# An interaction-network kernel with a tower: loads of the first chunk in order of use, dummy passes on TensorE, and the tower's first layer started inside the last tiles

## What is computed

```python
def cin(x0, filters):                      # x0: (512, 32 fields, 32 d)
    prev, outs = x0, []
    for W in filters:                      # (1, 32*32, 128), then (1, 32*128, 128)
        z = einsum('bhd,bmd->bhmd', x0, prev).reshape(b, h*m, d)
        prev = relu(einsum('bpd,pn->bnd', z, W[0]))
        outs.append(prev)
    return sum(concatenate(outs, axis=1), axis=-1)          # (512, 256)
e = stack([tbl_f[ids[:, f]] for f in range(32)], axis=1)
h = concatenate([cin(e, (filter_0, filter_1)), dense_ctx], axis=1)   # (512, 272)
h = maximum(h @ W_top1 + b_top1, 0)        # 512 wide
h = maximum(h @ W_top2 + b_top2, 0)        # 256 wide
y = h @ W_top3                             # (512, 1)
```

## Time and profile before

| | |
|---|---|
| median of 3 runs | 954.28 us (953.75 to 955.1) |
| the profiled execution, own time | 953.77 us |
| its span in the trace | 951.8 us |
| PE, DVE, ACT, POOL busy | 91%, 80%, 80%, 71% of the span |

### The profile page before, as it was taken

The page is one execution under the profiler, slowest core; times in us unless marked ns, Lnnn a source line. Parts: engine busy times, 40 slices in busy tenths (PEclk is TensorE's granted clock), DMA queues, the critical chain, the costliest instruction groups (busy, mean ns, idle before and its releaser), DMA issues.

```text
span 951.8 us, 14370 instructions
## 1 busy us (share of the span) xinstructions
PE 867.6 (91%) x3572; PEld 660.0 (69%) x3572; DVE 760.1 (80%) x2380; ACT 763.3 (80%) x2559; POOL 680.0 (71%) x650
## 2 busy tenths in 40 slices
PE   0326999999999999999999999989999999999997
PEld 0114777777777777767777777767777777777763
DVE  0123798896889999887888999978898899998882
ACT  1316998987888989888888898888888889989852
POOL 6772888786878888885788788865666666676560
PEclk9999999999999999999999999999999999999999
DMA  9045666666666666666666666666566666665430
GB/s 263 12 125 154 153 149 152 144 151 162 149 156 158 149 144 140 155 143 149 158 147 162 160 147 148 140 153 143 145 158 152 147 159 149 140 143 109 84 73 0
DMA packets 57718, 133.84 MB, mean 141 GB/s; under 512 B 8785, under 2 KB 22321, under 8 KB 57538
## 3 DMA queue, kind: packets, MB, share of 16 engines
q0 software_dynamic: 22528, 69.22, 38.8%
q1 hardware_dynamic: 32178, 59.94, 19.6%
q10 hardware_dynamic: 2928, 3.76, 1.3%
HBM read 62.64 MB, written 5.24 MB: 71 GB/s over the span
## 4 chain that ended last, share of the span: by engine, by line
PE 82%; issue 9%; POOL 3%; ACT 2%; DVE 2%; another core or an unknown queue 1%; DMA 1%; POOLq 0%; DVEq 0%; ACTq 0%
PE ya L651 15%; PE ya L652 13%; PE ya L653 13%; PE yd L651 10%; PE yd L652 10%; PE yd L653 10%; PE acc L652 3%; PE acc L651 3%; PE acc L653 3%; ACT scaled L439 1%; POOL quarter L305 1%; PE acc L674 1%; PE ya L750 1%; DVE acc L568 1%
## 5 line engine op out<-in xcount | busy, mean ns | idle before, releaser
L439 ACT ACTIVATE scaled<-ya,emb 128x128 f32<-128x128 f32 x2304 | 645.9, 386 | 91.8 <-PE ya L653 84.1
L568 DVE SCALAR_TENSOR_TENSOR acc<-yd,emb,acc 128x128 f32<-128x128 f32 x1408 | 394.7, 343 | 51.6 <-PE yd L653 51.4
L651 PE MATMUL ya<-w_hi,prev_hi 128*128 128x512 f32 x576 | 243.2, 422 | 11.0 <-DVE prev_lo L534 5.4
L305 POOL TENSOR_TENSOR quarter<-scaled 128x512 f32<-128x512 f32 x128 | 197.9, 1546 | 71.0 <-DMA scaled<-scaled 51.4
L652 PE MATMUL ya<-w_lo,prev_hi 128*128 128x512 f32 x576 | 227.4, 395 | 0.0
L653 PE MATMUL ya<-w_hi,prev_lo 128*128 128x512 f32 x576 | 226.8, 394 | 0.0
L298 POOL DMA_DIRECT2D scaled<-scaled x128 | 117.6, 919 | 119.3 <-ACT scaled L439 112.6
L651 PE MATMUL yd<-w_hi,prev_hi 128*128 128x512 f32 x448 | 176.7, 394 | 1.8 <-DVE pooled_b L587 1.5
L652 PE MATMUL yd<-w_lo,prev_hi 128*128 128x512 f32 x448 | 175.7, 392 | 0.0
L653 PE MATMUL yd<-w_hi,prev_lo 128*128 128x512 f32 x448 | 175.7, 392 | 0.0
L651 PEld LDWEIGHTS ya<-w_hi,prev_hi 128*128 128x128 f32 x576 | 108.6, 189 | 83.0 <-ACT scaled L439 37.8
(11 more groups left out here) (68 smaller groups left out, 719.9 us busy)
## 6 DMA issues: line engine op xcount, KB each, us to landing
scaled<-scaled POOLq DMA_DIRECT2D x128, 512.0 KB, 8.1
xb<-xt_scratch SPq DMA_DIRECT2D x64, 512.0 KB
x<-xt_scratch SPq DMA_DIRECT2D x64, 192.0 KB
xm<-xt_scratch SPq DMA_DIRECT2D x32, 256.0 KB
emb<-in_tbl,idx POOLq DMA_INDIRECT x128, 4.0
scaled<-in_L_rec_filter SPq DMA_DIRECT2D x8, 256.0 KB
xt_scratch<-xt_stage SPq DMA_DIRECT2D x7, 256.0 KB
xt_scratch<-xt_stage SPq DMA_DIRECT2D x9, 128.0 KB
```

Of the source, the lines that this page charges most:

```text
L305: pool.tensor_tensor(four, piece[:, 0:C], piece[:, C:2 * C], ALU.add).then_inc(quartered, 1)
L439: op = act.activation(scaled[:, tile % PR, C * j + N * i:C * j + N * (i + 1)], ya[:, n % RA, N * i:N * (i + 1)], ACT.Copy, scale=scale_of( ...
L568: dve.scalar_tensor_tensor(after, y_part, scale_of(tile, HB * j + i), before, ALU.mult, ALU.add).then_inc(chained, 1)
L651: pe.matmul(dst, v_hi, m_hi, start=start, stop=False)
```

## The change

Five edits:

1. SP's loads for chunk 0 are issued as `xm`, `xb` first half, `xb` second half, then `x16`. Chunk 1 and the later ones keep their order.
2. DVE and ACT do the four steps k of chunk 0 first and the small product after them; before, it stood between the first product and the first split.
3. PE issues 20 dummy passes of 512 columns (`WARM`) on weights that are already there, between the turning of the first batch and layer 0 of chunk 0. PE's waits for the later weights' low parts and for the context's share come ahead of them.
4. The tower's first layer is taken apart. The `pooled0` part goes into the extra round of the loop: two of its four products behind the last `yd` bank of tile 125, the other two behind the third of four `yd` banks of tile 126. Behind those come three of the four turns of `pooled1_b` and the `pooled1` products of 384 of the 512 columns. After the last tile only one turn, an ACT copy of 128 columns and four products of 128 columns are left.
5. The PSUM banks change: `tower_ps` is `ya` 0, `ya` 1, `xm_ps` and `prod`, and the second layer goes to `yd`.

```diff
@@ @block.sync
-            load_l0(0)
+            load_xm(0)
+            load_xb(0, 0)
+            load_xb(0, 1)
+            load_x16(0)
@@ @block.vector
-            product(0, 0)
+            for k in range(KT):
+                product(0, k)
+                split_low(0, k)
             first_small()
-            for k in range(KT):
-                split_low(0, k)
-                if k + 1 < KT:
-                    product(0, k + 1)
@@ @block.scalar
-            split_high(0, 0)
+            for k in range(KT):
+                split_high(0, k)
             small_high(0)
-            for k in range(1, KT):
-                split_high(0, k)
@@ @block.tensor, ahead of layer 0 of chunk 0
-            pe.wait_ge(w_lo_ready, 2)
+            pe.wait_ge(w_lo_ready, 4)
+            pe.wait_ge(ctx_share_ready, H1 // P)
+            for _ in range(WARM):
+                pe.matmul(yd[:, 0, :], w1_hi[:, 0, :], w1_hi[:, 0:HB, :], start=True, stop=True)
@@ @block.tensor, new functions
+            def tower_pooled0(q):
+                pe.matmul(tower_ps[q], wt1_sb[:, 0, P * q:P * (q + 1)], pooled0[:], start=True, stop=False)
+
+            def tower_pooled1(tiles, part_no):
+                pe.wait_ge(summed1, DC * CPB * tiles.stop)
+                for t in range(tiles.start, tiles.stop):
+                    turn = pe.transpose(acc0[:, P * t:P * (t + 1)], pooled1_b[:, t, :], identity[:])
+                turn.then_inc(pooled1_turned, 1)
+                pe.wait_ge(pooled1_ready, part_no)
+                for q in range(H1 // P):
+                    mm = pe.matmul(tower_ps[q][:, P * tiles.start:P * tiles.stop], wt1_sb[:, 1, P * q:P * (q + 1)],
+                                   pooled1[:, tiles, :], start=False, stop=part_no == 2)
+                    if part_no == 2:
+                        mm.then_inc(tower_mm, 1)
@@ @block.tensor, in the loop, behind bank_d(tile, j)
+                            if c == CHUNKS and q < 2 and j == 2:
+                                if q == 0:
+                                    pe.wait_ge(a_used, a_number(CHUNKS - 1, DC - 1, AQ[DC - 1] - 1) + 1)
+                                    pe.wait_ge(folded0, 2 * BT)
+                                    pe.wait_ge(summed0, CHUNKS)
+                                tower_pooled0(2 * q)
+                                tower_pooled0(2 * q + 1)
+                                if q == 1:
+                                    tower_pooled1(slice(0, BT - 1), 1)
@@ @block.tensor, after the loop
-            pe.wait_ge(summed1, TILES)
-            for t in range(BT):
-                turn = pe.transpose(acc0[:, P * t:P * (t + 1)], pooled1_b[:, t, :], identity[:])
-            turn.then_inc(pooled1_turned, 1)
-            pe.wait_ge(folded0, 2 * BT)
-            for q in range(H1 // P):
-                pe.matmul(tower_ps[q], wt1_sb[:, 0, P * q:P * (q + 1)], pooled0[:], start=True, stop=False)
-            pe.wait_ge(pooled1_ready, 1)
-            for q in range(H1 // P):
-                pe.matmul(tower_ps[q], wt1_sb[:, 1, P * q:P * (q + 1)], pooled1[:],
-                          start=False, stop=True).then_inc(tower_mm, 1)
+            tower_pooled1(slice(BT - 1, BT), 2)
```

More of the change, by code:

```diff
@@ L43, in cin_tower @@
     PR = 4
+    WARM = 20
     EARLY = 3 * F // 4
@@ L115, in cin_tower @@
         bt2_sb = sb("bt2_sb", [P, H2 // P])
-        tower_ps = [yd[:, 0, :], yd[:, 1, :], yd[:, 2, :], prod[:]]
+        tower_ps = [ya[:, 0, :], ya[:, 1, :], xm_ps[:], prod[:]]
         h1 = scaled[:, 0, 0:4 * C].rearrange("p (q c) -> p q c", q=4)
@@ L486, in _ @@
                                 split_high(c + 2, 0)
-            act.wait_ge(pooled1_turned, 1)
-            act.activation(pooled1[:], acc0[:].rearrange("p (t b) -> p t b", t=BT), ACT.Copy).then_inc(pooled1_ready, 1)
+            for k, tiles in enumerate((slice(0, BT - 1), slice(BT - 1, BT))):
+                act.wait_ge(pooled1_turned, k + 1)
+                act.activation(pooled1[:, tiles, :], acc0[:].rearrange("p (t b) -> p t b", t=BT)[:, tiles, :],
+                               ACT.Copy).then_inc(pooled1_ready, 1)
             for q in range(H1 // P):
@@ L494, in _ @@
             for q in range(H2 // P):
-                act.activation(h2[:, q, :], ya[:, q, :], ACT.Relu,
+                act.activation(h2[:, q, :], yd[:, q, :], ACT.Relu,
                                bias=bt2_sb[:, q:q + 1]).then_inc(tower_relu, 1)
@@ L702, in _ @@
             layer0_rest(0)
-            pe.wait_ge(w_lo_ready, 4)
-            pe.wait_ge(ctx_share_ready, H1 // P)
+            def tower_pooled0(q):
[11 more added lines that the diff above has]
+                        mm.then_inc(tower_mm, 1)
             for c in range(CHUNKS + 1):
@@ L749, in _ @@
                 for q in range(H2 // P):
-                    mm = pe.matmul(ya[:, q, :], wt2_sb[:, t, P * q:P * (q + 1)], h1[:, t, :],
+                    mm = pe.matmul(yd[:, q, :], wt2_sb[:, t, P * q:P * (q + 1)], h1[:, t, :],
                                    start=t == 0, stop=t == H1 // P - 1)
```

## The result

The changed kernel took 965.47 us (960.73 to 966.39, 5 runs) against 954.28 before: ratio 1.0107, 95% interval 1.0081 to 1.0134. It is slower by 1.1%, where 947.8 was forecast. The same kernel, unedited, was measured again in two later sessions, on two different chips (the chip of the first result is not on record), and took **950.15 and 949.20 us**, with ratios of 0.9969 and 0.9966 to the kernel before beside it. Both are results; most of this document is about what lies between them.

The account below looks back on a forecast made before the run. Passes on TensorE (busy 91%) set the even stretch's pace, so only start and end could move: 953.77 - 5.0 (start) - 1.5 (end) = 947.3, as median 947.8 us. The range was 944.6 to 951.4.

Parts of the forecast that it names:

- What is late next: Start, behind layer 0 of chunk 0: `x16(1)` limits ACT's first scaling, which comes at 77.3, 5.7 us earlier than 83.01.
- If the 3.8 us stay: Start: the unexplained wait before `prev_hi` remains, and ACT's first scaling could start at 76.7, `x16(1)` aside.
- if they go: Start: the unexplained 3.8 us before `prev_hi` vanish, and ACT's first scaling could start at 72.9, `x16(1)` aside.
- The clock: Start, on PE: a lower clock level loses 0.7 us (0 to 1.5); the 20 dummies cost nothing and gain nothing.
- the sum of the start: Start up to the first scaling: 5.7 us earlier less 0.7 for the clock, a gain of 5.0 us.
- Steps of chunk 0: Start: four products 2.1 us apart, loads in time, layer 0's last pass at 68.7 instead of 75.00, 6.3 us earlier.
- `x16(1)` as the limit: Start of chunk 1: the load is issued at 67.3, POOL's small product starts at 75.3 and sets the first scaling.
- First scaling: Start, on ACT: the first scaling comes at 77.3 instead of 83.01.
- The end: Last tiles and tower: DVE held up 4.1 us, second layer 2.2 us earlier, gain 1.5 us (0.1 to 2.6).
- one such stretch: End, second layer: one low-clock stretch from 934.8 loses 0.3 us of the 2.2 gained, a second another 1.7.
- Of the rivals, the second: Start and end: the 3.8 us go, `x16(1)` is quick, PE keeps the upper clock; 944.2 at the least, chance 0.12.
- Rival 5: End: inserted products meet PE's lower clock, DVE held up 13 us instead of 4.1, result 956.7; chance 0.04.

Follow-up runs that it names:

- e1: The changed kernel with no dummy passes (WARM = 0) instead of 20; 951.41 us, ratio 0.9958 to the kernel before.
- e14: The kernel before, unedited, measured again in the fourth session; 954.15 us, ratio 1.0010.
- e2: The kernel before with only the 20 dummy passes added, PE's two waits moved ahead of them; 959.46 us, ratio 1.0042.
- e15: The changed kernel without its dummy passes, measured again in the fourth session; 950.54 us, ratio 0.9973.
- e18: The kernel before with only the 20 dummy passes and the two moved waits, measured again in the fifth session; 950.92 us, ratio 0.9992.
- e13: The changed kernel, unedited, measured again in the fourth session; 950.15 us, ratio 0.9969.
- e7: The changed kernel with its 20 dummies, POOL's 22 early gathers of the second batch moved from the start to among the tiles; 967.0 us, ratio 1.0126.
- e8: The changed kernel without dummies, POOL's 22 early gathers of the second batch moved from the start to among the tiles; 965.65 us, ratio 1.0123.
- e6: The changed kernel with 5 dummy passes of 512 columns instead of 20; 957.57 us, ratio 1.0019.
- e12: The changed kernel with its 20 dummy passes moved earlier, to about 34 us, ahead of the first batch's turns; 951.05 us, ratio 0.9969.
- e17: The changed kernel, unedited, measured a third time, in the fifth session; 949.2 us, ratio 0.9966.
- e9: The changed kernel without dummies and without the context's part of the tower (24 PE instructions less); 949.8 us, ratio 0.9963.
- e16: The changed kernel with its 20 dummies at 34 us, ahead of the turns, measured again in the fourth session; 950.41 us, ratio 0.9968.
- e3: The kernel before with only edits 4 and 5 (the tower taken apart, its banks); 953.53 us, ratio 0.9975.
- e5: The changed kernel with its 20 dummy passes cut from 512 to 128 columns; 965.99 us, ratio 1.0120.

## Why the prediction was wrong

**The steps that failed** are three, and they lean on the same unread wait. The first is in "What is late next": from the last pass to `prev_hi` the chain showed 3.8 us "for which I see no cause", and the sum carried them along as a constant or dropped them ("If the 3.8 us stay", "if they go"). A third case was missing: that they grow. They were a late increment of PE, and in the session of the result the changed kernel met it at PE's first step, with 16.2 us. The second is in "The clock": the dummies "cost nothing, and cover is the 8.7 us in which PE has nothing to do". The cover was there (PE is idle from 55.57 to 60.72), but in sessions of that kind the dummies cost 14 us (after against e1), and five of them or 20 short ones also cost something, so what they cost was not PE's time. The third is the sum of the start, which takes 77.3 from the measured 83.01. In 83.01 itself some 2.6 us of the 3.8 were on the path, so that half of the 5.0 us counted as the change's gain was not its own; this shows in the sessions without late increments, below.

**Neither is a property of the changed kernel alone.** Shown: the same program has the 16.2 us in one session and none in two others; the kernel before has its 3.8 us in one and not in e14's, and e1 and e2 have late increments where e15 and e18, the same programs, have none. In the three sessions without late increments the dummies bring neither gain nor loss (e13 and e15 are 0.4 us apart, e18 is at 0.9992). In a session with them the lateness goes when POOL's early gathers are fewer (e7, e8). And all eight traces in which records of transfers are missing beside chunk 0's layer 0 (30 to 44 in 25 us, 1 to 3 of a landing's 16) have a late increment of PE there, though not each one is late (e1's second is in time). The twelve in which the record there is full have none: the ten of the last three sessions, and e7 and e8, whose gathers are over by then.

**What stays open** is what makes a session the one or the other. The first three sessions, in time (that of the result and the first two of the experiments), were of the late kind and the last three of the other, and the five of the experiments ran on five different chips, so chip, time and the manner of recording are not told apart. Single executions of the late sessions stand apart too (960.73 beside four above 965 in the first result, 952.8 to 959.36 in e6), and there is no trace of them. Nor can I say whether the thin record and the late increment have one cause. The Trainium skill ("NOTIFIC — the notification-queue block", section "Overflow: three behaviours, one of which stalls the engine") says that inside the block which writes such records the pipeline always holds its producers back rather than lose a record. Held-back producers would fit the late increments; the missing records they would not explain. No run here took the recording away: every execution with a time has a span and a granted clock on record. So it is an argument and not a finding, and it is open whether an execution without the recorder has the lateness at all. The row of counts by PE instruction (58 at 72.0, 62 at 74.6, 64 at 77.3) also fits, roughly, something released about once a gather; e12, meant as its test, ran in a session without lateness and tests nothing.

**Point by point, where increments were in time.**

- Steps of chunk 0: the last pass forecast for 68.7, at 67.81 in e13. `x16` and both halves of `xb` were there in time.
- `x16(1)` as the limit: issue forecast for 67.3 and POOL for 75.3; 66.40 and 75.42 in e13. That POOL's time agrees is in part luck: the load took 9.0 us from issue to use where the sum had 8.0, and e13's whole start stands 0.85 us earlier (first product at 57.40 instead of 58.25). With the old order of loads it took 9.4 to 10.6 us, with the new one 8.7 to 9.7, whenever it was issued (9.1 in after, issued at 82.69). The Trainium skill's rule of a leading broadcast ("DMA: Bandwidth & Descriptors", rules for kernel authors), that three copies outermost keep a transfer to at most three engines, is in line with so slow a load; no run here took the copies away, so it is not tested.
- First scaling: forecast 77.3; 77.24 in e13, 77.65 in e17. The start as a whole moves from execution to execution, so it is better counted from SP's issue of the first `xb` load: 30.6 us in before and 28.0 in e14, 27.9 in e18 (the old order), 25.5 in e13, 25.3 in e17 and 24.9 to 26.2 in the other four of its kind (e9, e12, e15, e16; the new one). So 2.6 of before's 3.8 us had been on the path, and the new order is worth 2.5 us, where the forecast had 5.0. The limit in e14 is `x16(1)` as well, issued at 69.80, and the change moves its issue by only 1 us against the first product.
- The end: here a size was off. Forecast gain 1.5 (0.1 to 2.6). Measured as the change of the stretch behind the last chunk's layer 0: 1.2 us in e1 and e3, 0.5 after, about 0.6 in e17, and a loss of 0.4 in e13. Over all traces the median of the stretch is 65.7 us in 15 with the new end and 66.2 in five with the old, so the gain is some 0.5. The hold-up of DVE and the early second layer are the same in all; the term that varies is the clock. The low stretch lasts 3.4 us in e1 and e3 and 6.8 in the other 13; with the old end it lasts 3.4 in four of the five. The forecast's 1.5 lies between what it had for one such stretch (1.9) and for two (0.2). In e13 it falls just before the second layer, for 6.8 us, which was in the bounds as two stretches, but all of it lands on the second layer: 10.02 us instead of 7.03, 3.0 lost where the bound had about 2.

```profile
924.68 0.87 DVE L573 SCALAR_TENSOR_TENSOR acc<-yd,emb,acc 128x128 f32<-128x128 f32 x3 [4.18 <-PE yd L656]
...
932.99 10.02 PE L768 MATMUL yd<-scaled,wt_sb 128*128 128x512 f32 x16 [0.84 <-ACT scaled L497]
```

```profile
core 0: us, PE busy (x) PEld busy (x) DVE busy (x) ACT busy (x) POOL busy (x), PEclk, DMA share, GB/s
924.00:932.00 8.00, 4.32 (x21) 2.90 (x19) 5.83 (x21) 0.28 (x1) 0.00 (x0) 1.00 0.00 1
932.00:938.80 6.80, 5.96 (x9) 2.52 (x8) 2.07 (x4) 2.42 (x4) 0.00 (x0) 0.50 0.00 0
```

These are e13's timeline and its windows of the end: PE waits 2.79 us for the last tile, and soon after that the level is 0.50 through nine of the 16 passes. e13's span is 4.4 us under e14's (952.3 and 947.9): 4.8 from the start less 0.4. Of the 4.8, 2.1 are not the change's: e14's first `xb` load is issued at 53.85 and e13's at 51.75, ahead of anything that the change touches but the dummies. The ratios say 3.0 us (0.9969) and 3.2 (0.9966), and this is what the parts give: 2.5 for the start and 0.5 for the end. Half of the forecast 6.5 is missing, 2.5 in the start and 1.0 in the end.

Of the rivals, the second let the 3.8 us go and none let them grow. Rival 5 had a loss, by a low clock at the inserted products; the clock there was 1.00 and DVE's hold-up 4.15 us, so its mechanism did not occur.

## What to carry to other kernels

A wait with "another core or an unknown queue" or "remote" as its releaser, in a kernel on one core, is a finding and not a constant. Look up when the awaited engine finished and when its increment is on record. Take out of the time that you compare with what of this wait lies on the path, and give the case in which the gap grows a price, before any edit that lets more work of that engine meet the gap. When edits are compared over several sessions, the unedited kernels belong into each of them; four edits in one session all looked like cures here. Count a start from an event that the change does not touch: the two starts compared here stood 2.1 us apart by themselves. Dummy passes were worth nothing here: the clock they raised had fallen again before the work came, so leave them out, or put them where nothing can queue behind them.

## What the runs showed of the hardware that was not expected

- PE's semaphore increments can be on record 16.2 us (19.1 in e5) behind the pass that makes them, and be waited for as long, while ACT's and DVE's own hand-overs beside them take 0.02 us. It was seen only beside GpSimd's gathers, issued 1.25 us apart, in three sessions, and not in three others. In the three with it, records of transfers are missing while the early gathers run (165 instead of 813 from 10 to 40 us in e7 against e13) and not behind them (190 and 191 from 50 to 75 us, e13's gathers not counted).
- The 20 dummies raise the granted clock to 1.00 at 51.4 us in e13, at 58.2 it is 0.50 again, and it stays there until 82.1, through all of chunk 0's layer 0. Without them (e15) it is 1.00 from 74.0 to 77.4 and then from 84.2 on, and the time is the same within 0.4 us.

```profile
51.40:58.20 6.80, 3.22 (x14) 2.29 (x13) 0.70 (x1) 0.67 (x2) 5.25 (x6) 1.00 0.76 238
58.20:82.10 23.90, 13.98 (x28) 8.36 (x29) 9.75 (x15) 8.94 (x22) 13.30 (x14) 0.50 0.50 144
```
